# Attention's row maxima carried in a spare row of the queries, ScalarE's list in a new order, and the first convolution's second half between transposed weights

## The reference, cut to what matters

```python
x = x + mamba(layernorm(x))            # in_proj, causal convolution of 4 taps, silu, dt, scan over time
x = x + xattn(layernorm(x), ctx, ctx, mask)
x = x + moe(layernorm(x))
# the part that the change touches
qh, kh, vh = heads(q @ w_q.T + b_q), heads(k @ w_k.T + b_k), heads(v @ w_v.T + b_v)   # 16 heads of 8
score = einsum('bhqd,bhkd->bhqk', qh, kh) / sqrt(8)
score = where(mask == 0, -1e9, score)      # mask: 256 queries x 64 keys
attn = softmax(score)
```

## Time and profile before

| | |
|---|---|
| median of 3 runs | 828.12 us |
| the profiled execution's own time | 829.39 us |
| its span, first to last instruction | 827.6 us |
| busy: PE, PEld | 686.6 us (83%), 479.3 us (58%) |
| busy: DVE | 684.4 us (83%) |
| busy: ACT | 523.0 us (63%) |
| busy: POOL | 618.9 us (75%) |
| mean granted TensorE clock | 0.936 |
| first scan, start of the last scan | 31.2 us, 602.0 us |

### The profile page before, as it was taken

The page is one execution under the profiler, slowest core; times in us unless marked ns, Lnnn a source line. Parts: engine busy times, 40 slices in busy tenths (PEclk is TensorE's granted clock), DMA queues, the critical chain, the costliest instruction groups (busy, mean ns, idle before and its releaser), DMA issues. The chain is left out here.

```text
span 827.6 us, 12373 instructions
## 1 busy us (share of the span) xinstructions
PE 686.6 (83%) x3923; PEld 479.3 (58%) x3923; DVE 684.4 (83%) x1043; ACT 523.0 (63%) x1223; POOL 618.9 (75%) x467
## 2 busy tenths in 40 slices
PE   6578667988898988889888888876679889999993
PEld 3444324556465655546555555554457678899993
DVE  3579999999999999999999999999963564765674
ACT  4677747887976878797687879567133433333345
POOL 1177988977999998999999999999771334675553
PEclk9779878999999999999999999989799999999997
DMA  4534785554648555544753663387254324787765
GB/s 106 205 116 120 211 257 176 164 176 148 190 139 223 167 167 177 181 143 128 224 165 105 193 192 118 114 224 219 69 160 155 126 97 140 249 297 235 228 240 152
DMA packets 80411, 142.70 MB, mean 172 GB/s; under 512 B 10555, under 2 KB 53574, under 8 KB 80346
## 3 DMA queue, kind: packets, MB, share of 16 engines
q1 hardware_dynamic: 75802, 133.38, 52.1%
q0 software_dynamic: 4544, 8.54, 2.9%
HBM read 110.25 MB, written 37.27 MB: 178 GB/s over the span
## 5 line engine op out<-in xcount | busy, mean ns | idle before, releaser
L1526 POOL TENSOR_TENSOR prod<-hst,BC 128x1024 f32<-128x1024 f32 x128 | 301.2, 2361 | 52.9 <-DVE hst L1741 41.8
L1741 DVE TENSOR_TENSOR_SCAN hst<-dA,Rp 128x1024 f32<-128x1024 f32 x128 | 292.3, 2283 | 9.0 <-ACT dA L1222 0.4
L1222 ACT ACTIVATE dA<-dtm,Aneg 128x255 f32<-128x255 f32 x512 | 213.9, 495 | 52.9 <-DVE hst L1741 52.1
L1531 POOL TENSOR_TENSOR prod<-prod 128x512 f32<-128x512 f32 x128 | 161.2, 1270 | 2.4
L1732 DVE TENSOR_TENSOR Rp<-BC,Rp 128x1024 f32<-128x1024 f32 x128 | 156.9, 1226 | 6.0 <-DMA BC<-bcd 0.6
L655 PE MATMUL Y<-prod,ident 128*128 128x256 f32 x512 | 140.5, 407 | 18.1 <-POOL prod L1531 14.6
L1649 POOL DMA_INDIRECT y2d<-prod,back x78 | 77.2, 989 | 97.5 <-DVE prod L2118 80.7
L655 PEld LDWEIGHTS Y<-prod,ident 128*128 128x128 f32 x512 | 101.2, 205 | 55.4 <-POOL prod L1531 20.3
L655 PE MATMUL Mb<-hpad,winT 128*128 128x512 f32 (+1 forms) x176 | 82.2, 615 | 14.7 <-ACT xh L1171 10.4
L1570 POOL DMA_INDIRECT xsd<-x2o,slots x64 | 63.1, 986 | 17.5 <-issue 16.8
L655 PEld LDWEIGHTS Rp<-BC,xh 128*128 128x128 f32 x608 | 73.6, 192 | 3.6 <-issue 1.8
(11 more groups left out here) (289 smaller groups left out, 1134.9 us busy)
## 6 DMA issues: line engine op xcount, KB each, us to landing
BC<-bcd SPq DMA_DIRECT2D x63, 1024.0 KB, 5.6
BC<-recs SPq DMA_DIRECT2D x39, 578.0 KB, 4.0
xsd<-blank SPq DMA_DIRECT2D x17, 1056.0 KB, 11.8
dtm<-xsd SPq DMA_DIRECT2D x39, 132.0 KB, 4.0
recs<-in_L_ffn_W SPq DMA_DIRECT2D x16, 256.0 KB
xin<-in_x SPq DMA_DIRECT2D x8, 256.0 KB, 5.2
x2d<-x2o SPq DMA_DIRECT2D x8, 256.0 KB, 5.6
E<-x2d SPq DMA_DIRECT2D x4, 512.0 KB, 5.4
```

Of the source, the lines that this page charges most:

```text
L1222: m = A(dA[:, k % RING, i, 1:SEQ], dtm[:, r % 2, d, b * SEQ + 1:(b + 1) * SEQ], ACT.Exp, scale=Aneg[:, d, c * NC + i:c * NC + i + 1])
L1526: TT(prod[:, k % RING, :, :], hst[:, k % RING, :, :], BC[:, (k // 2) % BCR, 1, :, :], ALU.mult).then_inc(s_pd, 1)
L1531: TT(prod[:, k % RING, 0:NC // 2, :], prod[:, k % RING, 0:NC // 2, :], prod[:, k % RING, NC // 2:NC, :], ALU.add).then_inc(s_fd, 1)
L1741: v.tensor_tensor_scan(hst[:, k % RING].rearrange("p n s -> p (n s)"), dA[:, k % RING].rearrange("p n s -> p (n s)"), U.rearrange("p n s - ...
```

## The change

Maxima. A query row `qT[:, w]` holds the heads of one parity and zeros elsewhere. The change puts the transposed maxima of the other parity's use into rows that are zero (four rows of each 32), and gives `Kbd` a second copy (index w) whose matching rows hold -1, so the float32 score matmul itself subtracts the maximum. `split_max`, `selmax`, `pickmax` and `nmT` go. `mx` is now 128 columns wide, zero outside the maxima; `turn_max` transposes it in float32 (4 transposes of 128x128), and `copy_max` copies it with 4 ACT operations of 32 partitions and 512 columns into `qT`. `Kbd` takes 8 ACT operations with a bias and a scale instead of 4 with a scale. The mask is transposed once (`turn_mask`, `copy_mask` in round 0) and each group of `scores_t` adds it with 4 bf16 matmuls instead of 8, and the 4 for the maxima go.

ScalarE's list. Several entries move, and with them `logits` on DVE from step 6 to step 5, `normed(1)` and `normed_input(1)` of round 0 from 5 to 6, and `att_variance` on PE in front of `gate_in`. `normalise` on DVE, and `att_out`, `mixer_out` and `scores_e` on PE, stay where they are.

Setup. `conv(0, 0)` and `conv(0, 1)` go into the transposes of the last weights, `silus(0)` in front of round 0. One DVE operation on `tri` goes, and the first steps of `attention_scale` and `routing_constants` are ordered anew.

```diff
@@ PE @@
-                pe.wait_ge(Tv.sem, Tv.at("me", r))
+                pe.wait_ge(Tv.sem, Tv.at("mx3b", r))
                 for i in range(NB * QT):
-                    m = pe.transpose(Tb[0:96, i * P:(i + 1) * P], nm[:, i, :, :], identb[:, :])
+                    m = pe.transpose(T[0][:, i * P:(i + 1) * P], mx[:, i, :], ident[:, :])
...
-                        mm(T[h][:, i * SEQ:(i + 1) * SEQ], Kbd[rows, b, 2 * g:2 * g + 2, :], qT[rows, i, b, :],
+                        mm(T[h][:, i * SEQ:(i + 1) * SEQ], Kbd[rows, i, b, 2 * g:2 * g + 2, :], qT[rows, i, b, :],
                            start=i == 0, stop=False, skip_group_check=True)
                 for i in range(2):
                     for h in range(2):
-                        o, hp = T[h][:, i * SEQ:(i + 1) * SEQ], TRIO[g][h][i]
-                        mm(o, selmax[:, hp, :], nmT[:, b * SEQ:(b + 1) * SEQ], start=False, stop=False, skip_group_check=True)
-                        for t in range(QT):
-                            m = mm(o[:, t * P:(t + 1) * P], mbias2[:, t, :, :], identb[:, :], start=False, stop=True,
-                                   skip_group_check=True)
+                        rows = slice(64 * h, 64 * h + 64)
+                        m = mm(T[h][:, i * SEQ:(i + 1) * SEQ], twice[rows, :, :], mbiasT[rows, :], start=False, stop=True,
+                               skip_group_check=True)
...
                     if k == (5 if r else 6):
                         conv(r + 1, 1)
+                        if prev:
+                            att_variance(r - 1)
                         gate_in(r + 1)
...
-                if prev and k == 5:
+                if prev and not nxt and k == 5:
                     att_variance(r - 1)
...
-            turn_weights(MIXER, NTURN)
+            turn_weights(MIXER, NTURN - 1)
+            conv(0, 0)
+            turn_weights(NTURN - 1, NTURN)
+            conv(0, 1)
@@ ACT @@
-            def silus(r):
+            def silus(r, between=False):
...
                 for d in range(DT):
+                    if between:
+                        key_half(r - 2, d)
                     act.wait_ge(Ap.sem, Ap.at(f"rs{d}", r))
                     A(sres[:, r % 2, d, :], M[d], ACT.Silu).then_inc(Aa.sem, 1)
...
+            def key_half(r, w):
...
+                for j in range(HP // 2):
+                    m = A(Kbd[:, w, :, j, :], KT[:, :, :], ACT.Identity, bias=kshift[:, w, j:j + 1], scale=kscale[:, w, j:j + 1])
...
             def copy_max(r):
                 act.wait_ge(Tp.sem, Tp.at("m", r))
-                A(nmT[:, :], Tb[0:96, 0:NB * SEQ], ACT.Copy).then_inc(Ta.sem, 1)
+                for w in range(2):
+                    for h in range(2):
+                        rows = slice(64 * h + 32 * (1 - w), 64 * h + 32 * (2 - w))
+                        m = A(qT[rows, w, :, :].rearrange("p b s -> p (b s)"), T[0][rows, :], ACT.Copy)
+                m.then_inc(Ta.sem, 1)
...
-                if prev and k == 5:
+                if prev and k == 3:
                     twice_contexts(r - 1)
-                if tail and k == 5:
+                if tail and k == 4:
                     att_out(r - 2)
                 if prev:
+                    if k == 4:
+                        mixer_out(r - 1)
                     if k == 5:
-                        mixer_out(r - 1)
-                    if k == 6:
+                        if tail:
+                            spreads(r - 2)
                         copy_kv(r - 1)
-                if tail and k == 6:
-                    spreads(r - 2)
-                if k == 6 and r < ROUNDS:
+                        att_square(r - 1)
+                if k == 6:
                     copy_xh(r, 1)
                 if prev and k == 6:
-                    key_blocks(r - 1)
-                    att_square(r - 1)
+                    if not nxt:
+                        key_blocks(r - 1)
+                    att_inverse_root(r - 1)
+                if k == 6:
+                    decays(r, 10)
+                if tail and k == 6:
+                    expert_exps(r - 2)
                 if nxt and k == (6 if r else 7):
-                    silus(r + 1)
-                if prev and k == 6:
-                    att_inverse_root(r - 1)
-                if tail and k == 7:
-                    expert_exps(r - 2)
+                    silus(r + 1, bool(r))
...
+                if ln and k == 14:
+                    inverse_roots_x(r + 2)
                 if prev and k == 14:
                     copy_max(r - 1)
-                if ln and k == 14:
-                    inverse_roots_x(r + 2)
-                if prev and k >= 14:
-                    exps(r - 1, 0, k - 14)
+                if nxt and k == 14:
+                    copy_xh(r + 1, 0)
+                if prev and k == 15:
+                    exps(r - 1, 0, 0)
+                    exps(r - 1, 0, 1)
...
+            copy_weights(MIXER, NTURN - 1)
             decays(0, 2)
-            copy_weights(MIXER, NTURN)
+            copy_weights(NTURN - 1, NTURN)
+            silus(0)
...
-                g = r * STEPS + k + 3
-                if g < ROUNDS * STEPS:
+                g = r * STEPS + k + (4 if 7 <= k < 13 else 3)
+                if k != 13 and g < ROUNDS * STEPS:
                     decays(*divmod(g, STEPS))
@@ DVE @@
-                if r and k == 14:
-                    v.wait_ge(Tv.sem, Tv.at("me", r - 1))
...
-            def split_max(r):
...
-                if r == 0 and k == 5:
+                if r == 0 and k == 6:
                     normed(1)
...
                 if tail:
-                    if k == 6:
+                    if k == 5:
                         logits(r - 2)
...
-                        split_max(r - 1)
...
-                    v.tensor_tensor(tri[:, :], tri[:, :], ident[:, :], ALU.subtract).then_inc(s_k, 1)
```

More of the change, by code:

```diff
@@ L185, in decoder @@
         KT = sb("KT", [P, NB, KEYS])
-        Kbd = sb("Kbd", [P, NB, HP // 2, KEYS])
+        Kbd = sb("Kbd", [P, 2, NB, HP // 2, KEYS])
         Vg = sb("Vg", [P, NB, HP, GW])
@@ L328, in decoder @@
         Ta = Marks(sem("Ta"), "KT V sq ln rs q m e00 e01 e10 e11 ld rd x2")
-        Tv = Marks(sem("Tv"), "xq " + " ".join(f"mx{i}a mx{i}b" for i in range(NB * QT)) + " ma mb mc md me n")
+        Tv = Marks(sem("Tv"), "xq " + " ".join(f"mx{i}a mx{i}b" for i in range(NB * QT)) + " n")
         s_kb = sem("s_kb")
+        s_mk = sem("s_mk")
         s_cT = sem("s_cT")
@@ L792, in scores @@
                         rows = slice(64 * h, 64 * h + 64)
-                        mm(T[h][:, w * SEQ:(w + 1) * SEQ], qT[rows, w, b, t * P:(t + 1) * P], Kbd[rows, b, :, :],
+                        mm(T[h][:, w * SEQ:(w + 1) * SEQ], qT[rows, 1 - w, b, t * P:(t + 1) * P], Kbd[rows, 1 - w, b, :, :],
                            start=w == 0, stop=False, skip_group_check=True)
@@ L1000, in _, with turn_mask @@
             mm(T[0][:, SEQ:SEQ + 1], attT[:, 3, :], bv[:, :]).then_inc(s_tr, 1)
+            def turn_mask():
+                pe.wait_ge(s_k, 3)
+                pe.wait_ge(s_cT, 2)
+                for t in range(QT):
+                    m = pe.transpose(Tb[:, t * P:(t + 1) * P], mbias2[:, t, :, :], identb[:, :])
+                m.then_inc(s_mk, 1)
             def first_round(k):
-                if k == 0:
-                    conv(0, 0)
-                    conv(0, 1)
                 if k == 1:
@@ L1260, in copy_kv @@
                 m.then_inc(Ta.sem, 1)
-            def key_blocks(r):
-                act.wait_ge(Ta.sem, Ta.at("KT", r))
-                if r:
-                    act.wait_ge(Tp.sem, Tp.at("st11", r - 1))
-                else:
-                    act.wait_ge(s_pre, NPRE + 6)
-                for j in range(HP // 2):
-                    m = A(Kbd[:, :, j, :], KT[:, :, :], ACT.Copy, scale=blk4[:, j:j + 1])
-                m.then_inc(s_kb, 1)
+            def key_half(r, w):
+                if w == 0:
+                    act.wait_ge(Ta.sem, Ta.at("KT", r))
+                    if r:
+                        act.wait_ge(Tp.sem, Tp.at("st11", r - 1))
+                    else:
+                        act.wait_ge(s_pre, NPRE + 12)
+                for j in range(HP // 2):
+                    m = A(Kbd[:, w, :, j, :], KT[:, :, :], ACT.Identity, bias=kshift[:, w, j:j + 1], scale=kscale[:, w, j:j + 1])
+                if w == 1:
+                    m.then_inc(s_kb, 1)
+            def key_blocks(r):
+                key_half(r, 0)
+                key_half(r, 1)
             def copy_max(r):
                 act.wait_ge(Tp.sem, Tp.at("m", r))
-                A(nmT[:, :], Tb[0:96, 0:NB * SEQ], ACT.Copy).then_inc(Ta.sem, 1)
+                for w in range(2):
[3 more added lines that the diff above has]
+                m.then_inc(Ta.sem, 1)
             def exps(r, b, g):
@@ L1317, in first_round @@
                 if k == 0:
-                    silus(0)
+                    copy_xd(0)
                 if k == 1:
```

(9 more changed lines are left out.)

67 lines of the change are left out of this document (31 added, 36 removed).

## The result

The changed kernel takes 846.77 us, the median of 4 runs (844.34 to 848.57), against 828.88 us for the kernel before: a ratio of 1.023, 95% interval 1.020 to 1.025. It is slower by 18 us, and outside the range of 819 to 834. The profiled execution took 846.93 us with a span of 844.8.

The account below looks back on a forecast made before the run. DVE was taken to bound the kernel from 31 to 604 us, PE after. Gains of 20.5 us against 18.6 lost gave -1.9: profiled execution 829.4 to 827.5 us, median 828.1 to 826.2, range 819 to 834.

Parts of the forecast that it names:

- Logits: DVE's logits in step 5 wait for PE: 2.8 us in rounds 2 to 6, 4.6 in round 7, 18.6 lost.
- slower rival: PE at its low clock every round, logits wait 4.1 us each: 25.1 lost, 832.7 us; chance 0.22.
- The split: Five small DVE operations behind each round's last maxima go: 1.42 us in rounds 1 to 7, 9.9 gained.
- ACT's list: ACT's copies, key blocks and new order: 3.5 us more work a round, costed at nothing against 15 us idle.
- thin spot: The softplus on ACT, read by DVE: its margin of 2.5 us was to fall to about 0.3.
- The share of idle time as cover: ACT's 3.5 us of added work a round set against its 15 us of idle time.
- Round 0: Setup: the scan of step 6 moves from 66.80 to about 60.2 us, 6.6 gained, bounds 3.3 and 7.
- first shift: Round 0: earlier silus(0) and no tri operation move step 3's scan and the norm up some 3.3 us.
- After the rounds: Around and after the last round, shorter transposed-score groups against longer copies and transposes: 2.0 us gained, bounds 0 and 4.
- Sum: Whole kernel: 20.5 us gained, 18.6 lost, -1.9 us; profiled execution 827.5 us, median 826.2.
- The test that I set: Forecast wrong if logits wait under 1 us, round 0 gains under 3, or new DVE waits for ACT pass 5.
- ACT becomes late: Rival: ACT late by more than 1 us a round at the softplus or queries, above 834 us; chance 0.03.

Follow-up runs that it names:

- e6: The kernel before with logits in step 5 on DVE instead of step 6, nothing else: 857.07 us, 1.033.
- e12: The kernel before without the split: float32 maxima turned to 16 rows, one ACT copy, subtracted by a float32 matmul: 966.44 us, 1.166.
- e3: The kernel after with the eight key-block operations behind the four silus instead of between them: 857.00 us, 1.034.
- e2: The kernel after with ACT's silus in front of the attention roots, decays(r, 10) and expert exponentials: 837.99 us, 1.012.
- e9: The kernel after, ACT's order kept, with four key operations instead of eight and one 96-row copy instead of four of 32: 841.83 us, 1.017.
- e17: e2 with idle matmuls on PE: 3 in front of gate_in, 5 behind turn_max, 2 in front of steps_in: 830.54 us, 1.003.
- e7: The kernel before with idle ACT work: four more key operations and three more 32-row copies: 859.80 us, 1.039.
- e10: The kernel before with three more idle 32-row copies on ACT in front of copy_max's one: 847.52 us, 1.022.
- e11: The kernel before with four more idle key operations on ACT in front of the four: 844.46 us, 1.020.
- e4: The kernel after with ACT's lists, logits' place and att_variance's place taken from the kernel before: 855.83 us, 1.032.
- e5: The kernel before with the setup part alone, including round 1's norm in step 6: 826.45 us, 0.997.
- e1: The kernel after with logits back in step 6 and ACT's spreads in step 6 in front of copy_xh: 843.11 us, 1.017.
- e8: The kernel after with the edits of e1 and e2 together: 838.22 us, 1.014.
- e18: e14 with idle matmuls on PE: 3 in front of gate_in, 5 behind turn_max, 2 in front of steps_in: 827.89 us, 0.999.
- e13: The kernel after with scores_e in front of att_out on PE: 847.29 us, 1.022.
- e14: e2 with scores_e in front of att_out on PE: 841.34 us, 1.015; its profiled execution took 832.25.
- e16: The kernel after with idle matmuls on PE: 8 in front of gate_in, 5 between turn_max and the transposed scores: 840.29 us, 1.014.
- e15: e14 with the second half of the key blocks behind the roots instead of between the silus: 842.00 us, 1.017.

## Why the prediction was wrong

- **Logits, right.** Forecast 18.6 us of waits; measured 3.14, 2.81, 2.64, 2.99, 2.99 and 4.14: 18.7. From the first matmul behind oT to the end of the last of the logits' it took 7.1 us at the full clock in round 4. My slower rival was wrong for this kernel and right about the place where the clock falls (the wait for the copies); in the old lists it came true (e6).
- **The split, right as far as rows go.** 9.9 us, by DVE's rows of round 4 in the kernel after. No run has it alone; e12 was meant to.
- **ACT's list, the step that failed.** I wrote "I cost it at nothing; if that cover is gone, at 1 us in each of 5 rounds", and named the softplus as the thin spot. The softplus was in time. The key blocks did fill waits for `gate_in`, as I said (e3). What I hadn't followed was what stands behind `gate_in` on PE: the sums of steps 4 to 7, for which `gate(r, 0)` waits. The roots, with 1.6 us of waiting for PE and 1.3 of work, 1.6 us of decays and 1.2 of expert exponentials in front of the silus made them late: 3.37, 1.36, 2.12, 1.98, 1.57 and 1.91 us in rounds 1 to 6, 12.3 in sum; with the silus in front (e2) they are gone, and with the added work left out and the order kept (e9) they are not. The sum also had no term for the clock: behind the longer wait `gate_in` took 3.78 us instead of 1.98, and that difference is as large as most of these waits. How the cost divides between the two isn't shown. e17, which keeps the terms of the forecast and has the silus first and the idle matmuls, takes 830.54 us, inside the range. I had seen that POOL's product of step 8 waits for PE's sum, and hid it behind `picks`; the same sums have a second reader on DVE. Maxima add 1.9 us of waiting for PE.
- **The share of idle time as cover.** "3.5 us more against 15 us of idle time" was the wrong comparison. e7, e10 and e11 put the price of ACT's work in front of the roots and of `copy_xh` at about its length or more. The old lists would have cost 27 us (e4). The four copies took 2.4 us (0.588 each) where I had 2.2.
- **Round 0, too large.** Forecast 6.6 us; the scan of step 6 started at 62.72 instead of 66.80, round 1's first `steps_x` 4.8 us earlier. But the first scan of all came 1.3 us earlier in this execution, and e5 has 2.6 us in all, by its ratio (0.7 to 4.4). The norm's place in step 6 worked. The first shift didn't come: DVE's wait in step 3 is 2.20 us, where the earlier trace rows had 1.80. Getting rid of the 2.26 us operation brought two others in its place (last section).
- **After the rounds.** Forecast 2.0 us; from DVE's norm of the first group of experts (line 2092 before) to the end it took 0.6 us less, and from the last scan to the end nothing less. The eight groups of transposed scores on the chain took 13.6 us instead of 18.6, as forecast: 2.5 each for the first two, with the clock at 0.64 in the mean of 614 to 624 us, and 1.28 for the last. (The first of them had taken 3.76 before, not 2.15.) But the copies take 1.8 us more each of the two times, and on the first chain one sum of the scan, 2.00 us at the low clock, now stands between the groups.
- **Sum.** The forecast for the profiled execution was 827.5 us. Add 12.3 for the gate, 1.9 for maxima, 0.1 for logits, 1.8 for round 0 and 1.4 behind the rounds: 845.0. It took 846.9; 1.9 us I don't place. The terms add waits of one execution, and e1 and e8 show that a wait taken away is not always a time won.
- **The test that I set.** I had looked for a new wait of DVE for ACT above 5 us. The new wait is for PE, and it is PE that waits for ACT. My rival "ACT becomes late", at a chance of 0.03, had the right side of the range, above 834, but its places, the softplus and the queries, were not where the time went.

No version beats the kernel before by more than a little: e5 by 0.3%, and e18 is level with it. That a version with a saving of 9.9 us on DVE is only level I put down to ACT's added work again: in e18 DVE waits 9.7 us for the roots and 6.2 for `copy_xh`, before 3.6 and 0.6. No run takes that work out of e18. Not tried is a form of the maxima that needs neither the split nor more of ACT.

## What to carry to other kernels

When work is put in front of an instruction, follow it through every engine's list to the next instruction that the bounding engine waits for; idle time in sum is no cover, only idle time between that pair is. When an engine's waits are removed one at a time, expect the next one on the same way to appear (e1, e8, e13), and look at TensorE's granted clock in the stretches before believing in a fixed ring (e14, e18), though the clock alone need not be it (e16). A reordering that costs time may be hiding a larger cost that it was made to avoid, so run the change without it (e4).

## What was not expected of the hardware

**Small DVE operations as long as POOL's.** In round 0 of the kernel after, timelines of DVE and of POOL:
```profile
32.33 0.17 DVE L1976 TENSOR_REDUCE quads<-blk 128x4 f32<-128x16 f32 x1
32.53 2.13 DVE L1977 TENSOR_TENSOR parity<-quads 128x2 f32<-128x2 f32 x1
...
40.27 2.29 DVE L1992 TENSOR_SCALAR first<-iota 128x8 f32<-128x8 f32 x1
```
```profile
32.30 2.35 POOL L1557 TENSOR_TENSOR prod<-hst,BC 128x1024 f32<-128x1024 f32 x1 [11.48 <-DVE hst L1771]
40.19 2.35 POOL L1557 TENSOR_TENSOR prod<-hst,BC 128x1024 f32<-128x1024 f32 x1 [5.54 <-DVE hst L1771]
```
Each ends within 0.03 us of POOL's product (34.65 and 42.54), which had started just before it. In the earlier trace rows it was the operation on `tri`. With that one gone, another stood beside POOL's second product, and what had been a wait of DVE for PE beside the first (2.1 us before) was an operation held as long. The Trainium skill ("SBUF — State Buffer", section Who interferes with whom) has a port pair that DVE and GpSimd hold by turns for a whole instruction; these rows agree. The reduction beside it, 0.17 us, wasn't held.

**Matmuls of few rows.** In e12 a float32 matmul of 16 rows and 256 columns takes 1.22 us at the low clock, and two of 128 rows just behind took 2.02. Four with 64 rows on two halves of the array took 2.08 us there, 0.52 each. The Trainium skill ("TensorE: Matmul & The Clock Gate", section Why this matters for your kernels) has a single matmul of few rows take as long as a full one, and the trace agrees. New is that the clock didn't rise through 29 us that were 96% busy, half of it with these matmuls. That it is they that kept it low is not shown.

**Equal periods.** In rounds 3 to 6 the kernel after, e1, e9, e13, e15 and e16 run at 74.9 to 75.5 us a round, with different work and waits. Each has the clock low in the same stretches of its rounds, but not for the same time: in round 4 for about 10 us in the kernel after, e1 and e13, 7 in e9, 16 in e15 and 4 in e16. So the low clock by itself doesn't set this period, and that they agree so closely isn't explained.
